# Row biases moved to quiet places of GpSimd, keys and values projected in another order over five buffers, last normalisation in four units

## The chip, the core and the metric

One NeuronCore of a Trainium2 chip runs the whole program. The metric is the device time of one execution in microseconds (us), median of three runs for the kernel before. Engines are named as the profile names them: PE is TensorE (matrix products), PEld its weight loads, DVE is VectorE, ACT is ScalarE, POOL is GpSimd, SP is the engine that only issues transfers. Each engine runs its own instructions in program order and waits on semaphores for the others.

## What is computed

Two decoder layers on x of 8 sequences, 100 tokens and 256 features, with a context of 8 times 361 rows. Each of the six blocks normalises x and adds its result to x:

```python
x = x + _L0_attn_ref(_layernorm(x), ...)     # block 0: attention ACROSS the 8 sequences, with CoPE positions
x = x + _L0_xattn_ref(_layernorm(x), ctx, ctx, ..., mask)   # block 1: single-head attention to the context
x = x + _L0_ffn_ref(_layernorm(x), ...)      # block 2: 8 experts, at most 100 tokens each, routed
x = x + _L1_attn_ref(_layernorm(x), ...)     # block 3: gated linear recurrence (a scan along the tokens)
x = x + _L1_xattn_ref(_layernorm(x), ctx, ctx, mask, ...)   # block 4: 16-head attention to the context
x = x + _L1_ffn_ref(_layernorm(x), weight)   # block 5: one product with a weight quantised to -1, 0, 1
```

The keys and values of block 4 depend on the context alone, not on x, so they can be computed at any time before block 4.

## The kernel before

Everything is written out by hand, one instruction stream per engine. `X` holds x as 100 token partitions by 8 sequences by 256; `XN` is its normalised copy, `XT` the transposed one. A normalisation is: statistics per sequence on DVE, `ve` = variance + eps on DVE, `rstd` by a power on POOL (`rsqrt`), `XN` on DVE (`norm`), transposes on PE (`transposes`), a copy to `XT` on ACT (`xt_out`). It runs in two groups of four sequences.

The row biases of blocks 0, 1, 3 and 4 are added to `X` on POOL (`bias`), and DVE adds each block's product after that (`add`).

The "side" work is the projection of block 4's keys and values: list `SIDE` gives its order, `SIDE_AT` says up to which item it has got at each named point of the program, and PE and ACT both walk the list (`side`). A key item ("k", b) is 8 matmuls of 361 columns on PE and 4 activations on ACT; then POOL splits the fp32 key into three bf16 parts (`split_key`, 3 operations), and SP stores them to `k_parts` in DRAM (`store_keys`). A value item ("v", b) is 12 matmuls and 2 activations. `k_buffer(b)` says in which SBUF buffer a key lies; a buffer is used again only when its stores have landed (`k_st`).

```python
SIDE = ([("qk", 0)] + [("k", b) for b in range(6)]
        + [("v", 0), ("k", 6), ("k", 7)] + [("v", b) for b in range(1, B)] + [("f", 0)])
SIDE_AT = {"cope": 1, "soft": 3, "ln1": 4, "b1_0": 5, "b1_2": 6, "b1_4": 7, "ln2": 8,
           "router": 9, "route": 12, "gather": 18}
```

So two keys are projected before the "spread" stage of block 0, one behind it ("ln1"), three inside the loop of block 1 ("b1_0", "b1_2", "b1_4"), and so on.

**The spread stage** (end of block 0) has 16 units u. For each, PE spreads the probabilities over the features (the product with `SELT`, 4 matmuls, line 1211), DVE multiplies by the values into `PB` (line 1660), and the sum over the 8 keys follows: on DVE for 11 units (`sum_keys`, line 484), on POOL for units 1, 4, 7, 10 and 13 (lines 706 and 707). When two units are summed, PE projects a sequence (`project0`), and DVE adds it to `X`. PE writes the spread products to `PP[u % 3]`, three pairs of PSUM banks.

**Block 1's loop** runs i from 0 to 10, a software pipeline: scores of i, transposes of i - 1, context product of i - 2, projection of i - 3, and then the side item of that i.

**Block 2** routes: POOL scatters the tokens to their experts' slots with 8 indirect transfers, SP loads the slots, PE runs the experts, SP stores `slots_out`, POOL gathers with 8 indirect transfers, DVE adds, and the normalisation for block 3 runs.

**Block 4** is driven by a table: `run_block4` walks ticks 0 to 171, and `PLAN` and `ONCE` say which piece each engine does at which tick; sequence b is 16 ticks behind sequence b - 1, and within a tick the pieces come in the sequence of `ORDER`. Block 5 follows as plain loops behind it.

## Time and profile before

| | us |
|---|---|
| median of three runs | 445.34 (443.82 to 445.56) |
| the profiled execution's own time | 443.37 |
| its span in the trace | 441.5 |
| PE busy | 407.4 (92% of the span) |
| DVE busy | 263.1 (60%) |
| ACT busy | 175.0 (40%) |
| POOL busy | 135.8 (31%) |
| mean granted TensorE clock | 0.973 of full |

The stages in the span: block 0 to its softmax until 64 us, the spread stage 64 to 113, block 1 until 164, routing until 190, the experts until 209, gather and normalisation until 228, block 3 until 322, block 4 until 428, block 5 until 441.5. A busy share is an average over all of these, so each stage has to be read by itself. A merged row of the timeline covers several like instructions: its start, its length from the first start to the last end, and in square brackets how long the engine was idle before and what released it.

### The profile page before, as it was taken

Reading aid. Unit: us, or ns where it says so; the run is one execution under the profiler, and the core shown is the slowest. Engines: PE = TensorE matmul, PEld = TensorE weight load, DVE = VectorE, ACT = ScalarE, POOL = GpSimd, SP = SyncE. Lnnn points to the kernel's source line nnn. Section 1 sums busy time; section 2 is a strip of 40 time slices with the busy share of each in tenths; the row PEclk is TensorE's granted clock in tenths of the full one; section 3 lists DMA queues with packets and bytes.
Section 4 is the critical chain, followed back from the end, with each engine's and each line's share of the span. In section 5 each row is a group of like instructions: output and inputs, shape, how many; then the busy total and the mean of one; then the engine's idle time right before and its main releaser. Section 6 shows DMA issues by size and latency. Waiting matters only on the chain.

```text
span 441.5 us, 7539 instructions
## 1 busy us (share of the span) xinstructions
PE 407.4 (92%) x2991; PEld 267.6 (61%) x2991; DVE 263.1 (60%) x473; ACT 175.0 (40%) x360; POOL 135.8 (31%) x183
## 2 busy tenths in 40 slices
PE   6999997894999999989979999999998999999976
PEld 2556754452656677658845555567765766666644
DVE  4149558499412363002379699995397677777324
ACT  0450450000443314523246585451205666666740
POOL 3830019332474300670562000000035473310100
PEclk9899999797899998999999999999999999999999
DMA  7994003000012279643210000018645446310002
GB/s 225 393 267 135 2 0 101 0 0 0 1 51 84 68 244 378 274 129 107 67 29 0 0 1 1 0 32 185 177 128 136 121 105 154 100 44 2 3 1 76
DMA packets 32850, 42.19 MB, mean 96 GB/s; under 512 B 7712, under 2 KB 29132, under 8 KB 32418
## 3 DMA queue, kind: packets, MB, share of 16 engines
q1 hardware_dynamic: 29897, 34.18, 25.5%
q0 software_dynamic: 2304, 5.76, 5.1%
q10 hardware_dynamic: 614, 1.77, 1.9%
q8 instruction: 24, 0.39, 0.4%
q14 instruction: 11, 0.09, 0.1%
HBM read 33.00 MB, written 8.98 MB: 95 GB/s over the span
## 4 chain that ended last, share of the span: by engine, by line
PE 61%; DVE 20%; issue 6%; ACT 5%; POOL 5%; DMA 3%; SPq 0%; POOLq 0%; DVEq 0%; ACTq 0%
PE banks L1073 6%; PE banks L1494 5%; PE banks L1479 4%; PE banks L1374 4%; PE banks L1448 4%; PE banks L1113 4%; PE banks L1135 4%; PE banks L1102 3%; DVE RA L484 3%; DVE NM L1848 2%; PE banks L1160 2%; PE banks L1244 2%; PE banks L1262 2%; PE banks L1342 2%; PE banks L1062 2%
## 5 line engine op out<-in xcount | busy, mean ns | idle before, releaser
L1848 DVE TENSOR_REDUCE NM<-banks 100x2 f32<-100x722 f32 x64 | 56.4, 903 | 19.4 <-PE banks L1448 19.1
L1342 PE MATMUL banks<-XT,RBG 128*128 128x400 f32 x192 | 65.0, 500 | 1.6 <-ACT XT L809 1.6
L1342 PEld LDWEIGHTS banks<-XT,RBG 128*128 128x128 f32 x192 | 36.3, 190 | 29.7 <-ACT XT L809 1.2
L1021 ACT ACTIVATE CT<-banks 128x400 f32<-128x400 f32 (+1 forms) x72 | 35.8, 504 | 23.2 <-PE banks L1479 21.7
L809 ACT ACTIVATE XT<-banks 128x800 f32<-128x800 f32 x10 | 8.3, 838 | 61.6 <-PE banks L1062 61.6
L1374 PE MATMUL banks<-W,RC 128*100 128x256 f32 x128 | 30.7, 380 | 0.6 <-DVE RC L1744 0.6
L752 POOL TENSOR_TENSOR rstd<-ve,mhalf 100x2 f32<-100x2 f32 x4 | 2.8, 702 | 88.2 <-DVE ve L1816 88.2
L1606 DVE TENSOR_TENSOR RC<-RV 128x800 f32<-128x800 f32 x16 | 15.6, 1022 | 16.1 <-ACT RV L851 14.1
L1211 PE MATMUL banks<-RC,SELT 128*128 128x400 f32 x64 | 24.3, 526 | 1.0 <-DVE RC L1646 0.7
L641 POOL TENSOR_TENSOR rstd<-ve,mhalf 100x4 f32<-100x4 f32 x10 | 10.6, 1065 | 46.3 <-DVE ve L1558 46.3
L1374 PEld LDWEIGHTS banks<-W,RC 128*100 128x100 f32 x128 | 21.0, 167 | 6.2 <-DVE RC L1744 1.0
L679 POOL TENSOR_TENSOR RA<-RA 128x722 f32<-128x722 f32 x6 | 9.1, 1510 | 49.5 <-ACT RA L831 49.5
L1102 PE MATMUL banks<-CT,W 128*128 128x361 f32 x64 | 23.2, 513 | 1.1 <-issue 1.1
L1494 PE MATMUL banks<-CT,RV 128*17 128x100 f32 (+1 forms) x576 | 24.0, 254 | 0.0
L1549 DVE BATCH_NORM_STATS2 st<-X 100x6 f32<-100x256 f32 x48 | 19.5, 423 | 7.0 <-DMA X<-in_x 5.9
L1120 PE MATMUL banks<-onesb 128*128 128x512 bf16 x81 | 21.4, 412 | 2.4 <-POOL onesf L629 2.4
L1113 PE MATMUL banks<-W,CT 128*128 128x256 f32 (+1 forms) x96 | 21.3, 380 | 0.5 <-DVE RC L1727 0.5
L1073 PE MATMUL banks<-W,RA 128*100 128x256 f32 x32 | 11.2, 485 | 10.6 <-DVE X L1588 6.1
L1727 DVE TENSOR_TENSOR RC<-banks,RC 100x256 f32<-100x256 f32 x8 | 3.4, 425 | 28.5 <-PE banks L1331 28.5
L1660 DVE TENSOR_TENSOR RC<-banks,RV 128x800 f32<-128x800 f32 x16 | 15.5, 977 | 7.6 <-PE banks L1211 7.6
L1113 PEld LDWEIGHTS banks<-W,CT 128*128 128x128 f32 (+1 forms) x96 | 17.5, 184 | 4.0 <-DVE RC L1727 0.9
L1211 PEld LDWEIGHTS banks<-RC,SELT 128*128 128x128 f32 x64 | 12.6, 201 | 11.0 <-DVE RC L1660 1.4
(244 smaller groups left out, 843.9 us busy)
## 6 DMA issues: line engine op xcount, KB each, us to landing
RA<-in_L_ffn_W SPq DMA_DIRECT2D x2, 2048.0 KB, 12.4
k_parts<-RA SPq DMA_DIRECT2D x18, 180.5 KB, 3.4
RBG<-in_L_attn_W_aiv SPq DMA_DIRECT2D x1, 3072.0 KB
CT<-in_ctx_t SPq DMA_DIRECT2D x2, 1444.0 KB, 11.4
RA<-k_parts SPq DMA_DIRECT2D x12, 180.5 KB, 3.4
RBG<-k_parts POOLq DMA_DIRECT2D x12, 180.5 KB, 4.3
RA<-k_parts POOLq DMA_DIRECT2D x12, 180.5 KB, 3.8
RBG<-in_ctx SPq DMA_DIRECT2D x2, 1024.0 KB, 17.5
```

The lines of the kernel that those rows point to most:

```text
L1021: sc.activation(P4[slot][0:n, g * HG * T:(g + 1) * HG * T], PS[4 + w % 2][0:n, 0:HG * T], ACT.Exp).then_inc(st_exp, 1)
L1073: ins = mm(bank[0:T, 0:D], lhs(k), rhs(k), start=(k == 0), stop=(k == KT - 1))
L1102: ins = mm((lo, hi)[m][:, 0:S], W4[:, 0, k, m * P:(m + 1) * P], CT[:, k, b * S:(b + 1) * S], start=(k == 0), stop=(k == KT - 1))
L1113: ins = mm(o, CT[:, k, b * S + s0:b * S + s0 + n], W4[:, 1, k, :], start=(k == 0), stop=(k == KT - 1))
L1120: mm(bank[:], onesb[:], onesb[:].unsqueeze(1).broadcast_to([P, 4, P]), start=True, stop=True)
L1135: ins = mm(PS[4 + i % 2][:, 0:GC], W0[:, w, k, m * P:(m + 1) * P], XT[:, k, GC * g:GC * g + GC], start=(k == 0), stop=(k == KT - 1))
L1211: ins = mm(PS[2 * (u % 3) + g][:, 0:GC], SELT[:, u], AL[:, GB * g:GB * g + GB].rearrange("p s t -> p (s t)"), start=True, stop=True)
L1342: ins = mm(PS[2 * aiv_pair(j, w) + g][:, 0:GC], WA[:, k, c:c + P], XT[:, k, GC * g:GC * g + GC], start=(k == 0), stop=(k == KT - 1))
L1374: ins = mm(PS[MIX_BANK[p]][0:T, b % 2 * D:b % 2 * D + D], UU[:, j, b, 1:TP], WMIX[:, j, :], start=(j == 0 and b % 2 == 0), stop=(j == RT - ...
L1494: ins = mm(PS[6][32 * c:32 * c + VW, g * T:g * T + T], V4[0:n, NJ * b + j, h, :], P4[(NJ * b + j) % PSLOTS][0:n, h * T:h * T + T], start=( ...
L1549: v.bn_stats(st6[:, b], X[:, b]).then_inc(stats_done, 1)
L1848: v.tensor_reduce(NM[:, b % 2, 2 * i:2 * i + 2], PP[w % 2][0:T, :, 0:S], AX.X, ALU.max, negate=True).then_inc(mx_out, 1)
```

## The change

- **Biases.** `bias(0)` is now issued on POOL ahead of the first `split_key`, where it was behind the second. `bias(3)`, one operation on 8 sequences, is now four on 2 sequences each, piece p behind the scan of feature group p (`state` at p + 1).
- **Side work.** All keys come first, then all values. There are five key buffers (`W0`'s space is the fifth), so four keys are ready before block 1. Keys 2 and 3 are projected in four halves inside the spread stage (`half_key`), in banks 4 and 5, which leaves the spread products two pairs of banks. Block 1's loop has no side item. The place of value 0 behind block 1 goes to key 5, the routing stage holds four values where it held two, and the gather four where it held five; 24 of 30 `keep_warm` matmuls in the routing stage go.
- **POOL's order.** In the spread stage `split_key(1)`, `(2)` and `(3)` stand between the sums. The power for the first group of block 3's normalisation stands ahead of the last gather.
- **SP's order.** The expert weights load when block 0 is done, where before six keys had to be stored; `WMIX` loads in the middle of the experts' stores.
- **Block 3's start.** PE transposes the second group after two of the three half products of the first group, not after three.
- **Last normalisation and block 5.** In four units of sequences, `LAST`, placed by tick in `ONCE`: the first six sequences' normalisation, transposes and part of the products lie inside block 4.

```diff
+LAST = [(0, 4), (4, 6), (6, 7), (7, 8)]
...
-        for r, at in ((SELT[:].rearrange("p a b -> p (a b)"), 0), (RC, 4600)):
+        for r, at in ((SELT[:].rearrange("p a b -> p (a b)"), 0), (RC, 4600),
+                      (W0[:].rearrange("p a k d -> p (a k d)"), 0)):
...
-        SIDE = ([("qk", 0)] + [("k", b) for b in range(6)]
-                + [("v", 0), ("k", 6), ("k", 7)] + [("v", b) for b in range(1, B)] + [("f", 0)])
+        SIDE = ([("qk", 0)] + [("k", b) for b in range(B)] + [("v", b) for b in range(B)] + [("f", 0)])
...
-        SIDE_AT = {"cope": 1, "soft": 3, "ln1": 4, "b1_0": 5, "b1_2": 6, "b1_4": 7, "ln2": 8,
-                   "router": 9, "route": 12, "gather": 18}
-        SIDE_LOW = [1, 9, 11, 13, 15]
+        SIDE_AT = {"cope": 1, "soft": 3, "spread": 5, "ln1": 6, "ln2": 7, "router": 8, "route": 13, "gather": 18}
+        SIDE_LOW = [1, 3, 4, 8, 10, 12, 14, 16]
+        SPREAD_AT = {4: (3, 0), 5: (3, 1), 9: (4, 0), 10: (4, 1)}
...
+                + [("last_norm", 142, 0), ("last_norm", 145, 1), ("last_tr", 146, 0), ("last_xt", 146, 0),
+                   ("last_mm", 150, 0), ("last_tr", 152, 1), ("last_xt", 152, 1), ("last_mm", 154, 1),
+                   ("last_mm", 162, 2), ("last_norm", 163, 2), ("last_tr", 169, 2), ("last_xt", 169, 2),
+                   ("last_mm", 169, 3), ("last_mm", 171, 4), ("last_norm", 171, 3), ("last_mm", 171, 5),
+                   ("last_mm", 171, 6), ("last_tr", 171, 3), ("last_xt", 171, 3), ("last_mm", 171, 7)])
...
+        K_BUFFER = (0, 1, 0, 1, 2, 3, 4, 2)
+        K_BEFORE = {2: 0, 3: 1, 7: 4}
...
-            for b in range(6):
+            for b in range(4):
                 store_keys(b)
...
-                sp.wait_ge(k_st[i], 16 * 3 * 3)
+                sp.wait_ge(k_st[i], 16 * 3 * 2)
...
-            sp.dma_start(WMIX, a["L1_attn_W_mix"].rearrange("(k p) n -> p k n", p=P)).then_inc(ld["wmix"], 16)
+            store_keys(4)
...
+            store_keys(5)
             sp.wait_ge(scat, 16 * B)
...
+                elif e == 4:
+                    sp.wait_ge(k_st[4], 16 * 3)
+                    sp.dma_start(WMIX, a["L1_attn_W_mix"].rearrange("(k p) n -> p k n", p=P)
+                                 ).then_inc(ld["wmix"], 16)
...
-            for b in range(2):
-                split_key(b)
             bias(0)
+            split_key(0)
 
             for i, u in enumerate(SUM_POOL):
...
+                if i == 0:
+                    split_key(1)
+                elif i in (1, 3):
+                    split_key(2 + i // 2)
...
-            split_key(2)
+            split_key(4)
             bias(1)
-            for b in range(3, 6):
-                split_key(b)
             rsqrt(2)
+            split_key(5)
...
-            rsqrt(3, 0)
+                if b == B - 2:
+                    rsqrt(3, 0)
...
-            bias(3)
+            for p in range(B // 2):
+                pool.wait_ge(xn_ready, 4 * B)
+                pool.wait_ge(state, p + 1)
+                gp.tensor_tensor(X[:, 2 * p:2 * p + 2], X[:, 2 * p:2 * p + 2],
+                                 RB[:, ROWBIAS[3]].unsqueeze(1).broadcast_to([T, 2, D]), ALU.add
+                                 ).then_inc(bias_added, 1)
...
+            def half_key(i, m):
+
+                b = SIDE[i][1]
+                if m == 0:
+                    pe.wait_ge(side_out, side_before(i))
+                for k in range(KT):
+                    ins = mm(PS[side_bank(i) + m][:, 0:S], W4[:, 0, k, m * P:(m + 1) * P],
+                             CT[:, k, b * S:(b + 1) * S], start=(k == 0), stop=(k == KT - 1))
+                if m == 1:
+                    ins.then_inc(side_mm, 1)
+                done[0] = SIDE_AT["spread"]
...
-                if u >= 3:
-                    pe.wait_ge(spread_used, u - 2)
+                if u >= 2:
+                    pe.wait_ge(spread_used, u - 1)
...
+                if u in SPREAD_AT:
+                    half_key(*SPREAD_AT[u])
...
-            keep_warm(PS[0], 30)
+            keep_warm(PS[0], 6)
...
-            transposes(3 * B, 1)
+                if n == 1:
+                    transposes(3 * B, 1)
```

PE's instructions in the spread stage of the kernel before; the product with SELT is line 1211, `project0` is the one with RA, and a key would be `CT,W`:

```order
L1211 MATMUL banks<-RC,SELT 128x400 x12
L1073 MATMUL banks<-W,RA 100x256 x2
L1211 MATMUL banks<-RC,SELT 128x400 x4
L1073 MATMUL banks<-W,RA 100x256 x2
L1211 MATMUL banks<-RC,SELT 128x400 x4
```

The same place in the changed kernel, where the spread product is line 1255 and a half key is line 1241:

```order
L1255 MATMUL banks<-RC,SELT 128x400 x10
L1241 MATMUL banks<-CT,W 128x361 x2
L1255 MATMUL banks<-RC,SELT 128x400 x2
L1105 MATMUL banks<-W,RA 100x256 x2
L1241 MATMUL banks<-CT,W 128x361 x2
L1255 MATMUL banks<-RC,SELT 128x400 x4
```

Keys 2 and 3 now stand between the spread products; each row counts instructions as written, of which PE runs two passes.

POOL's instructions at the same place before (line 679 to 681 is a key split, 669 the bias, 706 and 707 a sum):

```order
L696 TENSOR_SCALAR mk<-mk 8x361
L679 TENSOR_TENSOR RA<-RA 128x722
L680 CAST RA<-RA 128x722
L681 TENSOR_TENSOR RA<-RA 128x722
L679 TENSOR_TENSOR RA<-RA 128x722
L680 CAST RA<-RA 128x722
L681 TENSOR_TENSOR RA<-RA 128x722
L669 TENSOR_TENSOR X<-X,RB 100x2048
L706 TENSOR_TENSOR RC<-RC 128x400
```

And in the changed kernel (bias line 683, split 693 to 695, sum 719 and 720):

```order
L710 TENSOR_SCALAR mk<-mk 8x361
L683 TENSOR_TENSOR X<-X,RB 100x2048
L693 TENSOR_TENSOR RA<-RA 128x722
L694 CAST RA<-RA 128x722
L695 TENSOR_TENSOR RA<-RA 128x722
L719 TENSOR_TENSOR RC<-RC 128x400
L719 TENSOR_TENSOR RC<-RC 128x200
L720 TENSOR_TENSOR RA<-RC 128x100
L693 TENSOR_TENSOR RA<-RA 128x722
```

The bias now stands right behind the masks, and the first sum has one split ahead of it in place of two splits and the bias.

The end of PE's program before (1509 transposes the last attention output's sums, 1517 the output, 1073 with PEM is block 4's last projection, with WN block 5's):

```order
L1494 MATMUL banks<-SELT,RV 17x100 x16
L1509 MATMUL banks<-identf,WQK 100x113 x4
L1517 MATMUL banks<-identf,zrow 128x100 x2
L1073 MATMUL banks<-W,PEM 100x256 x2
L1062 MATMUL banks<-identf,XN 128x100 x8
L1073 MATMUL banks<-WN,XT 100x256 x8
```

And in the changed kernel (1582 is `last_tr`, 1597 `last_mm`):

```order
L1541 MATMUL banks<-SELT,RV 17x100 x12
L1556 MATMUL banks<-identf,WQK 100x113 x4
L1597 MATMUL banks<-WN,XT 100x256 x2
L1564 MATMUL banks<-identf,zrow 128x100 x2
L1582 MATMUL banks<-identf,XN 128x100 x2
L1597 MATMUL banks<-WN,XT 100x256 x2
L1105 MATMUL banks<-W,PEM 100x256 x2
L1597 MATMUL banks<-WN,XT 100x256 x6
L1582 MATMUL banks<-identf,XN 128x100 x2
L1597 MATMUL banks<-WN,XT 100x256 x2
```

Behind block 4's last projection stand four of block 5's eight products and one transposed sequence, where there were eight products and eight transposed sequences.

## Rows read from the trace of the kernel before

**Rows 1.** The page's chain that ended last, share by engine.

```profile
PE 61%; DVE 20%; issue 6%; ACT 5%; POOL 5%; DMA 3%; SPq 0%; POOLq 0%; DVEq 0%; ACTq 0%
```

**Rows 2.** Busy times by stretch: PE, PEld, DVE, ACT, POOL, then granted clock, DMA share, GB/s.

```profile
64.00:113.00 49.00, 37.41 (x114) 21.30 (x113) 41.07 (x58) 1.97 (x5) 23.87 (x23) 0.84 0.07 23
...
123.00:164.00 41.00, 40.26 (x215) 27.96 (x216) 15.65 (x48) 14.12 (x45) 16.16 (x11) 1.00 0.34 107
...
238.00:301.00 63.00, 62.60 (x197) 36.38 (x195) 58.03 (x62) 37.64 (x52) 0.00 (x0) 1.00 0.08 16
...
403.00:422.00 19.00, 18.18 (x317) 12.35 (x318) 7.10 (x18) 13.64 (x32) 1.83 (x5) 1.00 0.01 4
```

**Rows 3.** Timeline of the spread stage: start, length, engine, line, operation.

```profile
71.89 1.88 DVE L1660 TENSOR_TENSOR RC<-banks,RV 128x800 f32<-128x800 f32 x2
...
77.00 1.72 POOL L706 TENSOR_TENSOR RC<-RC 128x400 f32<-128x400 f32 x2
...
79.35 2.00 PE L1073 MATMUL banks<-W,RA 128*100 128x256 f32 x4 [4.51 <-POOL RA L707]
...
83.99 0.99 DVE L1660 TENSOR_TENSOR RC<-banks,RV 128x800 f32<-128x800 f32 x1 [5.53 <-PE banks L1211]
...
86.00 2.85 PE L1211 MATMUL banks<-RC,SELT 128*128 128x400 f32 x8
```

**Rows 4.** The chain that ended last, in block 1's loop: start, length, what.

```profile
124.91 2.62 PE banks L1102 x8
...
149.91 1.21 PE banks L1244 x4
...
154.02 1.21 PE banks L1244 x4
```

**Rows 5.** POOL beside DVE: two timeline rows, then single lines' durations (min/median/max ns).

```profile
64.05 1.56 POOL L679 TENSOR_TENSOR RA<-RA 128x722 f32<-128x722 f32 x1 [32.96 <-ACT RA L831]
...
64.62 1.84 DVE L1646 TENSOR_TENSOR RC<-RC,RA 128x800 f32<-128x800 f32 x1
...
L669 POOL TENSOR_TENSOR X<-X,RB x3: 4514/4530/4532, 72.5 to 230.0; 100x2048 f32<-100x2048 f32 x3
...
L1751 DVE TENSOR_SCALAR RA<-RA x10: 369/576/4540, 230.3 to 285.9; 128x800 f32<-128x800 f32 x6, 128x400 f32<-128x400 f32 x4
...
L1606 DVE TENSOR_TENSOR RC<-RV x16: 977/991/1271, 26.7 to 43.4; 128x800 f32<-128x800 f32 x16
...
L769 POOL TENSOR_TENSOR X<-X,RB x4: 1266/1270/1277, 336.0 to 356.4; 100x512 f32<-100x512 f32 x4
```

**Rows 6.** Timeline of one key activation on ACT, of the gather, and of block 3's start.

```profile
62.07 0.55 ACT L830 ACTIVATE RA<-banks,CB 128x361 f32<-128x361 f32 x1
...
209.53 13.22 PE L1113 MATMUL banks<-W,CT 128*128 128x256 f32 x60 [0.52 <-DVE RC L1727]
...
222.62 1.22 POOL L641 TENSOR_TENSOR rstd<-ve,mhalf 100x4 f32<-100x4 f32 x1
...
223.88 1.38 DVE L1563 TENSOR_SCALAR XN<-X,mv,rstd 100x256 f32<-100x256 f32 x4 [0.40 <-POOL rstd L641]
...
225.96 0.85 PE L1062 MATMUL banks<-identf,XN 100*128 100x100 f32 x8
...
233.84 16.39 PE L1342 MATMUL banks<-XT,RBG 128*128 128x400 f32 x48 [0.99 <-ACT XT L809]
```

**Rows 7.** Timeline of the end.

```profile
426.97 1.11 PE L1073 MATMUL banks<-W,PEM 128*100 128x256 f32 x4 [0.67 <-ACT PEM L1042]
...
428.12 0.42 DVE L1588 TENSOR_TENSOR X<-X,banks 100x256 f32<-100x256 f32 x1 [2.26 <-PE banks L1073]
...
435.13 3.70 PE L1073 MATMUL banks<-WN,XT 128*100 128x256 f32 x16 [0.99 <-ACT XT L809]
...
438.86 0.42 DVE L1588 TENSOR_TENSOR X<-X,banks 100x256 f32<-100x256 f32 x1 [0.44 <-PE banks L1073]
```

More of the change, by code:

```diff
@@ L241, in build @@
         fixed_st = sem("fixed_st")
-        k_st = [sem(f"k_st{i}") for i in range(4)]
+        k_st = [sem(f"k_st{i}") for i in range(5)]
         scat = sem("scat")
@@ L425, in run_block4 @@
                     for n, at, x in ONCE:
-                        if n == name and name in own and tick == at:
-                            own[name](x)
+                        if (n == name or n.startswith(name + "_")) and n in own and tick == at:
+                            own[n](x)
         def load_queries(queue, p, i):
@@ L586, in _ @@
             for i in (2, 3):
-                sp.wait_ge(k_st[i], 16 * 3)
+                sp.wait_ge(k_st[i], 16 * 3 * K_BUFFER.count(i))
             sp.wait_ge(fixed_st, 32)
@@ L795, in _ @@
                     bias_pair(3)
-            rsqrt(5)
+            for u, (b0, b1) in enumerate(LAST):
+                pool.wait_ge(unit_var, B // 2 + u + 1)
+                gp.tensor_tensor(rstd[:, b0:b1], ve[:, b0:b1], mhalf[:, 0:b1 - b0], ALU.pow).then_inc(unit_rstd, 1)
         @block.scalar
@@ L871, in _ @@
             side("soft")
+            side("spread")
             xt_out(xn_tr, G, xt_ready, [0])
@@ L1569, in after @@
                     return
+                if L == 4:
+                    last_stats(b)
+                    return
                 stats(L + 1, b)
@@ L1580, in after, with last_norm, last_stats @@
                     norm(L + 1, 1)
+            def last_norm(u):
+                dve.wait_ge(unit_rstd, B // 2 + u + 1)
+                for b in range(*LAST[u]):
+                    v.tensor_scalar(XN[:, b], X[:, b], mv[:, b, 0:1], rstd[:, b:b + 1], ALU.subtract, ALU.mult
+                                    ).then_inc(xn_ready, 1)
+            def last_stats(b):
+                stats(5, b)
+                if b >= 1 and b not in (b0 for b0, _ in LAST):
+                    aggregate(5, b - 1)
+                for u, (b0, b1) in enumerate(LAST):
+                    if b == b1 - 1:
+                        aggregate(5, b)
+                        dve.wait_ge(aggregated, 5 * B + b1)
+                        v.tensor_scalar(ve[:, b0:b1], mv[:, b0:b1, 1], EPS, None, ALU.add).then_inc(unit_var, 1)
             def add(L, b, bank):
@@ L1859, in normalise, with last_add @@
                                 ).then_inc(on_ready, 1)
+            def last_add(b):
+                dve.wait_ge(y5_mm, b + 1)
+                o = PS[(0, 1, 0, 1, 2, 3, 0, 1)[b]]
+                v.tensor_tensor(X[:, b], X[:, b], o[0:T, 0:D], ALU.add).then_inc(x_final, 1)
             run_block4(maxima=row_max, normalise=normalise, add=lambda b, _: add(4, b, Y4), x_add=x_add,
-                       zero_bank=zero_bank, ln_stats=ln_stats, ln_norm=ln_norm)
-            for b in range(B):
-                add(5, b, PS[4 + b % 4])
+                       zero_bank=zero_bank, ln_stats=ln_stats, ln_norm=ln_norm,
+                       last_mm=last_add, last_norm=last_norm)
 _OUT = (B, T, D)
```

106 lines of the change are left out of this document (64 added, 42 removed).

## The prediction

> **What bounds the kernel now.** I read the chain that ended last first, since a busy share of 92% for PE says nothing about one stage. It gives PE 61% and DVE 20%, with ACT and POOL at 5% each [rows 1]. The stretches [rows 2] then show four different limits. In the spread stage (64 to 113 us) DVE is busy 41.1 of 49 us, PE 37.4, at a granted clock of 0.84. In block 1's loop (123 to 164) PE is busy 40.3 of 41 and DVE 15.7: whatever leaves PE there shortens the program. In block 3 (238 to 301) DVE is busy 58.0 of 63 and is the limit that its own order sets. In block 4's tail (403 to 422) PE is busy 18.2 of 19 and ACT 13.6.
>
> The spread stage has one hole [rows 3]. POOL's first sum starts only at 77.00, behind two key splits and the bias. PE needs that sum for its first projection, so it sat idle 4.51 us until 79.35. When it came back, that projection took 2.00 us for four matmuls, against 3.70 for sixteen at the full clock [rows 7]: after the idle time the clock stood at the lower of its levels. DVE waited 5.53 us in all, until 83.99, for unit 6.
>
> **Spread stage, 3.0 us less.** The first sum now has one split ahead of it; three operations of at most 1.56 us [rows 5] are 4.7 us, and they start at the same 64.05, so POOL is free at about 68.7, and the sum of unit 1 follows its product at about 70.5. A sum takes 1.72 plus some 0.4 us [rows 3]. It is ready at about 72.6, before PE asks. What is late next is PE's queue, which now holds half keys, and with two pairs of banks it may start unit u only when unit u - 2 has been read. Unit 2 is read at 71.89 + 0.94 = 72.8 [rows 3]. Behind it on PE: unit 4 (1.4, half of 2.85 [rows 3]), half a key (1.3, half of 2.62 [rows 4]), unit 5 (1.4), the projection (0.93, a quarter of 3.70 [rows 7]), half a key (1.3), unit 6 (1.4). Together 7.7 us, so DVE gets unit 6 at about 80.7 and not at 83.99: 3.3 us earlier. In the rest of the stage DVE needs 2.4 to 3.3 us per unit, PE at most 1.4 + 1.3 + 0.93 = 3.6 with a half key and 2.4 without, so PE keeps up but for some 0.3 us at units 10 to 12. The other splits (4.7 us each) stand between sums that are 7 us apart. I take 3.0. Bounds: 5.5, the whole wait, and 0, if PE's queue or its clock eats it.
>
> **Block 1, 7.4 us less.** Three keys leave the loop; in the chain they stand as rows of line 1102, the first 2.62 us and two more of 2.45 and 2.43 [rows 4]. PE is the limit there, and a step without a key takes 154.02 - 149.91 = 4.11 us, of which the profile shows PE at work nearly throughout. Hence all three count, less 0.1. What DVE and ACT do per step is far below 4 us (15.7 and 14.1 of 41 [rows 2]). The bias of block 1 takes 4.5 us on POOL behind one split; DVE wants it at step 3, some 7 us behind step 0, and it starts before step 0: still covered. Bounds: 7.5, and 5 if the short first steps, which have little PE work, turn to waiting on ACT's exponentials.
>
> **Behind block 1, 0.4 us more.** Key 5 stands where a value stood. Its four activations take 0.55 each [rows 6], at most 2.2 us, and the copy of `XT` for the router queues behind them on ACT; a value has two. Between 0 and 1.2; I take 0.4. The two further values in the routing stage, 2.6 us each (13.22 / 5 [rows 6]), take the place of 24 warming matmuls and lie in the wait for the scattered slots: nothing.
>
> **Gather to block 3, 1.6 us less.** One value fewer frees PE 2.6 us earlier. The next limit is the normalisation: XN's first group is written from 223.88 to 225.26, PE transposed it from 225.96 [rows 6]. The power waited on POOL behind the last gather and started at 222.62; ahead of it, it may start up to 0.5 earlier. So transposes at about 224.8, 1.1 us earlier. The second group's transposes now come one half product sooner, and that half product covers ACT's copy, for which PE sat 0.99 us [rows 6]; against it the last gather starts 1 us later. I count 0.5 net. Bounds: 0 and 2.6. `WMIX` (1 MB) now goes ahead of the last expert stores in SP's queue. In block 1 the transfers made 107 GB/s at a share of 0.34, so some 315 GB/s are possible and it takes 3.3 us, with two pairs of experts still to be computed behind its issue: 0.2 us, bounds 0 and 3.3.
>
> **The biases, 1.5 us more.** POOL and DVE do disturb each other. At 64.05 POOL starts a 1.56 us subtraction, and DVE's product at 64.62 takes 1.84 us where 0.99 is usual [rows 5]: it ends 0.85 us behind POOL's end at 65.61, as if it had stood still until then. The clamp of line 1751, 369 ns at best, once took 4540 ns, when the 4.53 us bias of block 3 ran [rows 5]. That wait disappears, but ACT's table loads were the limit at that time, so it gives nothing. The four new pieces, 1.27 us each [rows 5], start when a scan ends; one product later (about 1 us, as at 83.99 [rows 3]) DVE runs an operation with both inputs in SBUF, which would stand for 0.3 to 0.4 us. Four times: 1.2 us taken, bounds 0 and 1.7. The bias of block 0 now runs beside the sixteen multiplications of line 1606, 0.99 us each, from 26.7 [rows 5]. A full stop costs DVE 4.5 us, but its five buffers put it four units (3.9 us) ahead of PE, which leaves 0.3 us taken, bounds 0 and 1.0 if the lead isn't full.
>
> The Trainium skill ("SBUF — State Buffer", section "Who interferes with whom") says of this that a VectorE instruction with two SBUF inputs contends with a GpSimd instruction that reads SBUF, and that the one that starts first holds the shared port for its whole length. By that rule, this change puts four pieces and one whole bias beside just such instructions, and the trace agrees in the row at 64.62.
>
> **The end, 2.8 us less.** Now 441.5 - 428.12 = 13.4 us pass from the last addition of block 4 to the end [rows 7], with eight products (0.93 each) and two copies in between. In the changed kernel the path is: addition 0.42, statistics to variance some 0.8, power at most 1.2, one normalised sequence 0.35 (a quarter of 1.38), transposes 0.2, copy some 0.5, product 0.93, with handovers about 4.6 us to the last addition, whose start stood 2.6 us before the end [rows 6, 7]. That is 7.2: 6.2 us less. Against this, transposes and products move ahead into a stretch where PE is busy 18.2 of 19 us: two transposes (0.85 and about 0.4) and two products (0.93 each) are 2.9 us more, and in the gaps of the last sequence (0.67 us before 426.97 [rows 7]) a third and a fourth product overrun by 0.5. Net 2.8. Bounds: 5 (ACT is the true limit in that tail and PE's additions hide) and 0.
>
> **Sum.** -3.0 - 7.4 + 0.4 - 1.6 + 0.2 + 1.5 - 2.8 = -12.7 us. The profiled execution took 443.4, so 430.7; the median of the runs shown is 2.0 above it, so about 432.5.
>
> **Rivals.** (A) The forecast, 0.63. (B) Block 1's loop doesn't get its 7.4 us back, because the shortened steps wait for ACT and DVE: 4 us are lost, 436.5. For it: step i + 1 needs step i's exponentials. Against it: PE is at work 40.3 of 41 us there [rows 2]. 0.1. (C) The port: the pieces of the biases, and the splits that now lie beside DVE's work, stop DVE at each meeting, with their bounds (1.7 + 1.0) and another 1.5 in the router: 435.5. This is the skill's rule at full price; the row at 64.62 speaks for it, the 1606 line, whose longest is 1271 ns beside two POOL operations, against it. 0.12. (D) More than forecast: the end gives 5 and the spread stage 4.5: 428.5. For it, the better clock once the idle 4.5 us is gone (0.84 now). 0.12. (E) Slower than before: the two bank pairs tie PE to DVE's reads, PE gets a pause in each unit, and its clock stays at the lower level for the stage. PE needs 35 us there at full speed (37.4 less what the low clock added, plus 5.2 for the keys); at half speed up to 70, against 49 in all. To lose the other 10 us it must run over 23 us of the stage slow. The one fall seen came behind a pause of 4.5 us, and the new queue has none over 1 us: 0.03, 447 or more.
>
> **Numbers.** 432.5 is A's. Its own range, 429.5 to 435.5; with B, C and D the range is 428 to 437. Differences under 0.5% (2.2 us) can't be told from no change: faster 0.95, same 0.02, slower 0.03.
>
> **What would show it.** Spread stage: no PE wait over 1 us before unit 6, DVE's wait there some 2.2 us, clock above 0.95. Block 1's loop: 33.6 us where it took 41. Line 1751's longest near 0.6 us, and four of DVE's line-1775 products at 1.3 us or more. From block 4's last addition to the end 7.2 us. The prediction is wrong if PE waits for ACT in block 1's first steps, if the experts' last store lands late behind `WMIX`, or if block 4's tail grows by more than 3.4 us.

## The result, and the profile after

The changed kernel took 439.2 us (median of 4 runs, 437.58 to 443.51); the kernel before, beside it, 445.45 us. The ratio is 0.9866, with a 95% interval of 0.9831 to 0.9901. The forecast was faster, which holds (by 1.3%), by 12.7 us, which doesn't: some 6 us came. The profiled execution took 437.58 us with a span of 435.8, against 443.4 and 441.5 before, so the two traces differ by 5.7 us, and that is what has to be divided up. Executions of one kernel fall into a fast and a slow state: ratios use the fast ones alone and medians all of them, and the traces of experiments 2 and 3, which are of slow ones, are read for single stretches only.

The windows of the changed kernel, over the stretches that answer to those of [rows 2] (mean granted clock, then DMA share and GB/s, stand last):

```profile
62.00:111.00 49.00, 42.32 (x139) 24.30 (x138) 43.43 (x61) 8.98 (x18) 26.97 (x28) 0.97 0.15 46
120.00:154.00 34.00, 32.83 (x191) 23.29 (x192) 15.53 (x48) 8.80 (x33) 4.86 (x2) 1.00 0.20 59
232.00:294.00 62.00, 60.83 (x192) 35.34 (x190) 56.04 (x56) 36.09 (x50) 5.09 (x4) 1.00 0.09 18
398.00:422.00 24.00, 22.10 (x360) 15.33 (x361) 8.67 (x22) 15.72 (x36) 2.74 (x6) 1.00 0.03 7
```

The spread stage has its clock back (0.97 for 0.84), and block 1's loop takes 34 us for 41 with PE nearly as full as it was (32.8 of 34 us, 40.3 of 41). To see where the rest went, I took one event at each border in both traces and subtracted:

| stretch, up to | before, us | after, us | change | forecast |
|---|---|---|---|---|
| DVE's reduction of block 0's logits | 59.24 | 60.15 | +0.9 | +0.3 |
| last spread product | 105.25 | 103.09 | -3.1 | -3.0 |
| first scores of block 1 | 123.19 | 120.64 | -0.4 | 0 |
| last projection of block 1 | 163.33 | 153.44 | -7.3 | -7.4 |
| first gather | 212.32 | 202.87 | +0.4 | +0.6 |
| first full product over the scans (line 1775, now 1862) | 242.03 | 234.21 | +1.6 | -1.6 |
| last scan | 299.32 | 292.94 | +1.4 | +1.2 |
| last addition of block 3 | 337.0 | 332.2 | +1.6 | 0 |
| end | 441.5 | 435.8 | -0.9 | -2.8 |

The two large terms are right to 0.1 us. Of the 7.0 us that are missing, 3.2 went between the gather and block 3, 1.6 at block 3's end, 1.9 in the tail, 0.6 in block 0; the other rows give 0.3 back.

**The hole in the spread stage**, in the changed kernel's timeline (answers to [rows 3]):

```profile
71.48 1.72 POOL L719 TENSOR_TENSOR RC<-RC 128x400 f32<-128x400 f32 x2 [1.92 <-DVE RC L1747]
77.84 1.03 PE L1105 MATMUL banks<-W,RA 128*100 128x256 f32 x4
81.46 0.99 DVE L1747 TENSOR_TENSOR RC<-banks,RV 128x800 f32<-128x800 f32 x1 [2.02 <-PE banks L1255]
```

POOL's first sum starts at 71.48 and no longer at 77.00, PE's projection waits for nothing and takes 1.03 us for four matmuls instead of 2.00, and DVE waits 2.02 us for unit 6, where it waited 5.53.

**Between gather and block 3** (answers to [rows 6]):

```profile
212.81 1.04 POOL L655 TENSOR_TENSOR rstd<-ve,mhalf 100x4 f32<-100x4 f32 x1 [0.98 <-DVE ve L1625]
213.89 3.38 DVE L1630 TENSOR_SCALAR XN<-X,mv,rstd 100x256 f32<-100x256 f32 x4
214.08 1.18 POOL L748 DMA_INDIRECT XN<-slots_out,small  x1 [0.23 <-issue]
214.36 0.72 PE L1094 MATMUL banks<-identf,XN 100*128 100x100 f32 x4 [2.44 <-DVE XN L1630]
215.44 1.69 POOL L761 MEMSET CT<- 128x808 f32 x2
216.47 0.39 PE L1094 MATMUL banks<-identf,XN 100*128 100x100 f32 x2 [1.40 <-DVE XN L1630]
219.00 5.28 PE L1388 MATMUL banks<-XT,RBG 128*128 128x400 f32 x8 [0.22 <-ACT XT L833]
```

Four normalisations that took 1.38 us took 3.38; PE waited 2.44 and 1.40 us in its transposes, and its next 8 multiplications took 0.66 us each, where those of before took 0.36 (4.27 us for 12).

**Block 3 and its end.** Source line 1862, one of POOL's pieces, and PE where the last scan releases it:

```profile
L1862 DVE SCALAR_TENSOR_TENSOR RC<-RA,RC x4: 999/1178/1361, 244.9 to 290.9; 128x808 f32<-128x808 f32 x4
269.89 1.27 POOL L768 TENSOR_TENSOR X<-X,RB 100x512 f32<-100x512 f32 x1 [6.60 <-DVE RC L1831]
270.65 1.36 DVE L1862 SCALAR_TENSOR_TENSOR RC<-CT,RC 128x808 f32<-128x808 f32 x1
294.83 6.25 PE L1421 MATMUL banks<-W,RC 128*100 128x256 f32 x20 [2.00 <-DVE RC L1831]
```

Half of the eight products took 1.36 us, as forecast. New is the last row: PE sat idle for 2.00 us and then took 6.25 us for 20 matmuls that had taken 4.56. The same row before, line 1374 there, has a pause of 0.62 us:

```profile
301.21 4.56 PE L1374 MATMUL banks<-W,RC 128*100 128x256 f32 x20 [0.62 <-DVE RC L1744]
```

**The tail** (answers to [rows 7]; rows of PE):

```profile
417.63 1.11 PE L1597 MATMUL banks<-WN,XT 128*100 128x256 f32 x4
421.84 1.11 PE L1597 MATMUL banks<-WN,XT 128*100 128x256 f32 x4
426.80 1.03 PE L1597 MATMUL banks<-WN,XT 128*100 128x256 f32 x4
427.67 1.03 PE L1105 MATMUL banks<-W,PEM 128*100 128x256 f32 x4
432.04 1.11 PE L1597 MATMUL banks<-WN,XT 128*100 128x256 f32 x4 [0.43 <-ACT XT L1075]
```

Block 4's last product (line 1105) now comes at 427.67, behind a product of block 5 at 426.80. From it to the end 8.2 us pass, where it was 14.6; but from block 3's last addition to it 95.5 us pass, where it was 90.0.

### The profile page after: what moved, and what is told of

Read it like the earlier page. It is cut to its first block, busy times and chain, and to the rows that moved or that the text cites. A ratio compares the mean times of both kernels' runs of the same rounds, so it can differ in the third digit from the quotient of the medians.

```text
span 435.8 us, 7507 instructions
## 1 busy us (share of the span) xinstructions
PE 405.3 (93%) x2967; PEld 265.5 (61%) x2967; DVE 267.7 (61%) x475; ACT 174.9 (40%) x362; POOL 137.1 (31%) x188
## 4 chain that ended last, share of the span: by engine, by line
PE 56%; DVE 22%; issue 7%; DMA 5%; ACT 5%; POOL 3%; SPq 1%; POOLq 0%; DVEq 0%; ACTq 0%
PE banks L1421 5%; PE banks L1541 4%; PE banks L1105 4%; PE banks L1167 4%; PE banks L1526 4%; PE banks L1495 3%; PE banks L1255 3%; DVE NM L1934 3%; PE banks L1192 3%; PE banks L1388 2%; PE banks L1290 2%; PE banks L1308 2%; DVE RA L493 2%; DVE RC L1862 2%; DVE RC L1828 2%
## 5 line engine op out<-in xcount | busy, mean ns | idle before, releaser
L1388 PE MATMUL banks<-XT,RBG 128*128 128x400 f32 x192 | 67.3, 513 | 0.2 <-ACT XT L833 0.2
L1388 PEld LDWEIGHTS banks<-XT,RBG 128*128 128x128 f32 x192 | 37.4, 196 | 29.6 <-issue 3.1
L1421 PE MATMUL banks<-W,RC 128*100 128x256 f32 x128 | 32.3, 395 | 2.0 <-DVE RC L1831 2.0
L1693 DVE TENSOR_TENSOR RC<-RV 128x800 f32<-128x800 f32 x16 | 19.3, 1278 | 14.2 <-ACT RV L875 14.2
L655 POOL TENSOR_TENSOR rstd<-ve,mhalf 100x4 f32<-100x4 f32 x8 | 8.5, 1057 | 47.8 <-DVE ve L1625 47.8
L768 POOL TENSOR_TENSOR X<-X,RB 100x512 f32<-100x512 f32 x4 | 5.1, 1272 | 45.5 <-DVE RC L1831 45.5
L1152 PE MATMUL banks<-onesb 128*128 128x512 bf16 x57 | 16.7, 435 | 2.4 <-POOL onesf L643 2.4
L1134 PE MATMUL banks<-CT,W 128*128 128x361 f32 x48 | 17.7, 521 | 1.1 <-issue 1.1
L1526 PE MATMUL banks<-RC,RA 100*128 100x100 bf16 (+1 forms) x192 | 16.6, 210 | 1.3 <-DMA RC<-NT 1.3
L833 ACT ACTIVATE XT<-banks 128x800 f32<-128x800 f32 x8 | 6.6, 841 | 27.9 <-PE banks L1094 27.9
```

Source lines behind the costliest of these rows:

```text
L1134: ins = mm((lo, hi)[m][:, 0:S], W4[:, 0, k, m * P:(m + 1) * P], CT[:, k, b * S:(b + 1) * S], start=(k == 0), stop=(k == KT - 1))
L1388: ins = mm(PS[2 * aiv_pair(j, w) + g][:, 0:GC], WA[:, k, c:c + P], XT[:, k, GC * g:GC * g + GC], start=(k == 0), stop=(k == KT - 1))
L1421: ins = mm(PS[MIX_BANK[p]][0:T, b % 2 * D:b % 2 * D + D], UU[:, j, b, 1:TP], WMIX[:, j, :], start=(j == 0 and b % 2 == 0), stop=(j == RT - ...
L1526: ins = mm(PS[4 + w % 2][0:n, c * T:c * T + T], KS[b % KSLOTS][0:KROWS, h, s0:s0 + n], queries(KROWS, h, b), start=True, stop=True)
L1693: v.tensor_tensor(PB[u % 5], k0[:, k].rearrange("p (s t) -> p s t", s=B), q0[:, k, s * T:s * T + T].unsqueeze(1).broadcast_to([P, B, T]), ...
```

## The experiments

Each kernel is the changed one with the edit shown. I read the local stretch from its trace first, since single edits are worth 1 to 3 us and the executions of one kernel lie up to 15 us apart. Each experiment has one trace.

**1. PE kept busy ahead of the transposes** (439.2 became 438.3; ratio to before 0.9885, 0.9809 to 0.9960)

```diff
-            keep_warm(PS[2], 5)
+            keep_warm(PS[2], 17)
```

> The changed kernel with 17 warming matmuls, where it has 5, ahead of the transposes of XN's first group between the gather and block 3; nothing else. In the changed kernel PE stopped at 211.9, waited 2.44, 1.40 and 0.46 us in and before those transposes, and then took 5.28 us for the first 8 multiplications of W_aiv (0.66 each, where 0.356 is the pace of the kernel before: 4.27 us for 12). Theory 'the clock': what lowered it is the idle 2.4 us, so with it filled the first 8 take 2.9 to 3.3 us and the whole comes 2 us earlier (437.2 where the changed kernel took 439.2). Theory 'the normalisation': the 1.40 and 0.46 us inside the transposes are enough to keep the clock low, or the first half of W_aiv isn't on the path: the 8 still take over 4.5 us or the median stays within 0.5 us of 439.2.

```profile
214.25 3.38 DVE L1630 TENSOR_SCALAR XN<-X,mv,rstd 100x256 f32<-100x256 f32 x4
219.36 3.65 PE L1388 MATMUL banks<-XT,RBG 128*128 128x400 f32 x8 [0.22 <-ACT XT L833]
293.57 4.56 PE L1421 MATMUL banks<-W,RC 128*100 128x256 f32 x20 [2.01 <-DVE RC L1831]
```

The 8 multiplications take 3.65 us, the normalisation 3.38 as without the edit, and from the first gather to the first full product 29.8 us pass, not 31.3: this much of the clock's share is worth 1.6 us. It is not all of it: the granted clock was still 0.50 from 217.4 to 220.8, and the 8 took more than the 2.9 to 3.3 us that were expected. The median says nothing at this size. The third row is a warning: the pause at block 3's end is there as in the changed kernel, and this time the clock held.

**2. The power behind the last gather** (436.7 us; 0.9761, 0.9692 to 0.9831)

```diff
-                if b == B - 2:
-                    rsqrt(3, 0)
+            rsqrt(3, 0)
```

> The changed kernel with the power of block 3's first group back behind POOL's last gather, as it stood in the kernel before. In the changed kernel the four normalisations of that group took 3.38 us from 213.89, where 1.38 is usual, with the last gather's issue (1.18 us) and two memsets (1.69 us) on POOL at the same time. Theory 'POOL stops DVE, gather first': without the gather beside it the group takes 1.4 to 1.8 us and is ready at 216.2 or earlier, in place of 217.27; the transposes end 1 us earlier, and the median falls by 0.5 to 1 us. Rival 'the memsets do it': they now begin right behind the power and lie beside the whole group; it takes 2.5 us or more and nothing is won, or 0.3 us lost.

```profile
217.54 2.56 DVE L1629 TENSOR_SCALAR XN<-X,mv,rstd 100x256 f32<-100x256 f32 x4 [0.40 <-POOL rstd L655]
217.65 1.67 POOL L760 MEMSET CT<- 128x808 f32 x2
```

Without the gather beside it the group still takes 2.56 us, with the memsets at the same time: that is what the rival expected of the group. Its price was wrong, though: the stretch is 30.1 us and not 31.3 or more.

**3. The memsets behind the normalisation** (432.7 us; 0.9748, 0.9699 to 0.9798)

```diff
+            pool.wait_ge(xn_ready, 3 * B + GB)
             gp.memset(DEC[:, :, :, 0:1], 0.0)
```

> The changed kernel with POOL's memsets ahead of block 3 behind the normalisation of XN's first group, and nothing else. Of the stretch from the first gather to DVE's first full-width scan product (31.3 us; 29.7 before) the warming alone took 1.6 us away, the power alone 1.2, all three edits 4.0. If the three add up, this one takes 1.2 us away: 30.1 us, the four normalisations 2.4 us or less where they took 3.4. Rival 'the gather's issue is what stops DVE, the memsets only follow it': they still take over 3 us, and the three edits gave more together than apart because only together do they leave the clock up.

```profile
213.78 1.42 DVE L1631 TENSOR_SCALAR XN<-X,mv,rstd 100x256 f32<-100x256 f32 x4
213.89 1.22 POOL L748 DMA_INDIRECT XN<-slots_out,small  x1 [0.23 <-issue]
215.12 0.47 DVE L1819 SCALAR_TENSOR_TENSOR X<-XN,small,X 100x256 f32<-100x256 f32 x1
215.52 1.65 POOL L762 MEMSET CT<- 128x808 f32 x2
216.72 4.62 PE L1389 MATMUL banks<-XT,RBG 128*128 128x400 f32 x8 [0.64 <-ACT XT L834]
```

No expectation had this: the group takes 1.42 us beside the gather's issue, so without the memsets nothing holds it, and one wait is worth 3.0 us (28.3 for 31.3) even with the clock still low in the last row. The three edits overlap, they don't add up. One detail stays open: in the changed kernel the third of the four normalisations is recorded from 214.54 to 216.42, and the first memset only from 215.27. That taking the memsets away frees it is shown; why it stood 0.7 us ahead of them is not.

**4. All three, with 20 warming matmuls** (431.4 us; 0.9710, 0.9665 to 0.9755)

> The changed kernel with three edits between the gather and block 3: the power of XN's first group behind the last gather, POOL's five memsets behind that group's normalisation, and 20 warming matmuls instead of 5. Nothing is then beside the normalisation, and PE has no pause. With the power alone moved, the normalisation took 2.56 us; with the warming alone, 1.6 us of this stretch came back. Theory 'two causes, POOL beside the normalisation and PE's clock': the four normalisations take 1.4 us and the 8 multiplications behind them 2.9 us; from the first gather to DVE's first full-width scan product (line 1862) 28.0 to 28.8 us pass, where the changed kernel took 31.3 and the one before 29.7. Rival 'one cause is all': 29.5 to 29.9, as with the warming alone.

```profile
214.56 1.38 DVE L1630 TENSOR_SCALAR XN<-X,mv,rstd 100x256 f32<-100x256 f32 x4 [0.40 <-POOL rstd L655]
217.47 2.92 PE L1388 MATMUL banks<-XT,RBG 128*128 128x400 f32 x8 [0.64 <-ACT XT L833]
```

Both at full speed, and 27.3 us for the stretch: 4.1 less than in the changed kernel, 2.4 less than before, where the forecast said 1.6. Each edit alone leaves 1.0 to 2.8 us of that.

**5. Block 3's bias whole again** (433.8 us; 0.9777, 0.9722 to 0.9832). One operation over all sequences at its old place instead of the four pieces.

> The changed kernel with block 3's bias as one operation of 4.5 us at its old place, and not as four pieces behind the scans. In the changed kernel four of DVE's products of line 1862 took 1.37 us where 1.00 is usual (1.44 us in all), DVE's last scan ended 6.38 us earlier than before and PE's multiplications 7.77 us earlier, PE then sat idle for 2.00 us at 292.83 and took 6.25 us for 20 matmuls of W_mix (4.56 before). Theory 'the pieces cost twice': they delay DVE by 1.4 us, which opens PE's pause, which lowers its clock: without them the products take 1.00 us, the pause is 0.6 us, the clock in that stretch 1.0, and the median falls by 2.5 to 3 us. Rival 'the clock falls for itself': 1.4 us are won and the 20 matmuls still take over 5.5 us. Rival 'the whole bias costs as much': the clamp waits up to 4.5 us for it and ACT's table loads no longer hide it: less than 1 us is won.

```profile
L1859 DVE SCALAR_TENSOR_TENSOR RC<-RA,RC x4: 999/999/999, 243.3 to 287.8; 128x808 f32<-128x808 f32 x4
291.73 4.56 PE L1418 MATMUL banks<-W,RC 128*100 128x256 f32 x20 [0.60 <-DVE RC L1828]
```

All products take 1.00 us, the pause is 0.60 and the 20 matmuls 4.56. From the first full product to block 3's last addition 94.9 us pass (232.6 to 327.5), where it was 98.0: 3.1 us, twice what the pieces cost DVE. The clamp took 4.09 us once and cost nothing, hidden under ACT's table loads as forecast.

**6. The bias of block 0 earlier** (441.6 us; 0.9906, 0.9866 to 0.9946). `bias(0)` ahead of the wait for the masks.

> The changed kernel with the bias of block 0 ahead of POOL's wait for the masks, where POOL sat idle for 5.47 us (20.99 to 26.46), and not beside the sixteen multiplications of line 1693. Theory 'the bias stops DVE': the multiplications' mean falls from 1278 ns to 1000 to 1080, the chain up to the spread stage ends 0.5 to 0.9 us earlier, and the median falls by as much. Rival 'the second mask operation and the earlier start of the key splits do it': the mean stays above 1200 ns with the bias away. A third outcome: the row biases' transfer lands later than 21, and the bias still meets the multiplications.

```profile
27.36 5.09 POOL L683 TENSOR_TENSOR X<-X,RB 100x2048 f32<-100x2048 f32 x1 [5.55 <-DMA BR<-in_L_ffn_br]
L1693 DVE TENSOR_TENSOR RC<-RV x16: 975/978/5315, 26.2 to 44.6; 128x800 f32<-128x800 f32 x16
```

The third outcome: the row biases' transfer held POOL until 27.36, and the bias met the multiplications all the same. But the second row shows what a meeting is: one multiplication of sixteen took 5.3 us, and the median 978 ns. It is recorded from 27.98 to 33.30, and the bias ends at 32.45: DVE isn't slowed, it stands until POOL has finished and ends 0.85 us later.

**7. Block 5 back behind block 4** (440.2 us; 0.9910, 0.9871 to 0.9949). The last units undone, the rest as changed.

> The changed kernel with one part undone: block 5's normalisation, transposes and products stand behind block 4 in two groups of four, as in the kernel before; the rest is as changed. The last units put five PE steps ahead of block 4's last product (420.31, 427.67) and shortened what follows its addition from 13.4 to 7.0 us. Theory 'the tail is PE's': those steps each cost their full time (0.87, 0.93, 0.56, 0.93, 1.0 us; by the two traces 5.1 us lost against 6.4 won), so with the part undone the tail from block 4's last product to the end is 14.5 us again, block 4 ends 4 to 5 us earlier, and the whole ends 1.3 us later than the changed kernel, as it did in the profile. Rival 'the forecast': the part is worth 2.8 us, and the 1.08 us that PE waited for a transfer of the maxima has nothing to do with it: 2.5 to 3 us later.

```profile
422.14 1.11 PE L1091 MATMUL banks<-W,PEM 128*100 128x256 f32 x4 [0.67 <-ACT PEM L1060]
430.29 3.70 PE L1091 MATMUL banks<-WN,XT 128*100 128x256 f32 x16 [0.99 <-ACT XT L826]
```

From block 3's last addition (331.4) to block 4's last product 90.7 us pass, 95.5 in the changed kernel; from there to the end (436.7) 14.6 for 8.2. So the units lose 4.8 and win 6.4: 1.6 us net in these two traces, between the two expectations. PE's waits for the maxima's transfers are in it, 0.4 us here and 1.3 in the changed kernel; without them the net is 2.5.

**8. Eight pieces, and the end reordered** (436.7 us; 0.9831, 0.9772 to 0.9890)

```diff
-            for p in range(B // 2):
...
+            for b in range(B):
+                pool.wait_ge(state, b + 1)
+                ins = gp.tensor_tensor(X[:, b], X[:, b], RB[:, ROWBIAS[3]], ALU.add)
...
-                   ("last_mm", 162, 2), ("last_norm", 163, 2), ("last_tr", 169, 2), ("last_xt", 169, 2),
-                   ("last_mm", 169, 3), ("last_mm", 171, 4), ("last_norm", 171, 3), ("last_mm", 171, 5),
-                   ("last_mm", 171, 6), ("last_tr", 171, 3), ("last_xt", 171, 3), ("last_mm", 171, 7)])
+                   ("last_norm", 162, 2), ("last_mm", 162, 2), ("last_tr", 169, 2), ("last_xt", 169, 2),
+                   ("last_mm", 171, 3), ("last_mm", 171, 4), ("last_norm", 171, 3), ("last_mm", 171, 5),
+                   ("last_tr", 171, 3), ("last_xt", 171, 3), ("last_mm", 171, 6), ("last_mm", 171, 7)])
```

> The changed kernel with two edits far apart. (1) Block 3's bias in eight pieces of one sequence each (0.64 us), one behind each scan, and not four of 1.27 us. DVE's operation right behind a scan reads a PSUM bank and took 0.96 us beside a piece as without one; the product of line 1862 comes 0.91 us behind the scan and was held until the piece's end. Theory 'DVE stands until POOL's operation ends, and only where both its inputs are in SBUF': a piece of 0.64 us ends before it, all eight products take 1.00 us, PE's pause is 0.6 us and the 20 matmuls behind it 4.56. Rival 'any meeting costs': the products or the scans take 0.2 us or more longer. (2) At the end, block 5's fourth product behind block 4's last and not ahead of it, and the normalisation of the third unit ahead of the third addition. Expected: block 4's last product (427.67 there) 0.8 us earlier against block 4's eighth reciprocal, and the end 0.8 us nearer; the rival says the products behind it then hold the last unit's transposes and nothing is won.

```profile
268.29 0.96 DVE L1860 TENSOR_TENSOR RC<-RC,banks 128x800 f32<-128x800 f32 x1
268.46 0.73 POOL L768 TENSOR_TENSOR X<-X,RB 100x256 f32<-100x256 f32 x1 [6.79 <-DVE RC L1831]
269.29 1.00 DVE L1862 SCALAR_TENSOR_TENSOR RC<-CT,RC 128x808 f32<-128x808 f32 x1
293.12 4.56 PE L1421 MATMUL banks<-W,RC 128*100 128x256 f32 x20 [0.59 <-DVE RC L1831]
```

A piece of 0.73 us ends at 269.19 under DVE's operation on a PSUM bank, and the product behind it takes 1.00 us: the same bias, in smaller pieces, is free. At the end 7.7 us pass from the last reciprocal (421.25) to the last addition (428.97), where it was 8.3: 0.6 us won of 0.8.

**9. All edits** (428.1 us; 0.9631, 0.9582 to 0.9680). Experiments 4 and 8, and `bias(0)` behind `pool.wait_ge(pos_ready, 1)`.

> Everything that the runs so far point to: the gather edits (power, memsets, warming), block 3's bias in eight pieces, the end's two edits, and the bias of block 0 behind DVE's sum over the gates (about 52 us), where DVE's operations read PSUM banks, and not at 30 us, where it stopped one multiplication of line 1693 for 5.3 us. Against the changed kernel I expect 0.9 us from the bias of block 0 (0 if DVE's operations at 52 to 57 stop too), 2.5 to 3 from the gather stretch, 1.4 and the 1.6 of the low clock from block 3's bias, 0.8 from the end: 6 to 7.5 us, so 432 to 433.5 us. If the theory of two causes is wrong at any of these places, the trace shows it there.

```profile
L1694 DVE TENSOR_TENSOR RC<-RV x16: 978/988/1266, 26.7 to 43.4; 128x800 f32<-128x800 f32 x16
51.24 0.99 DVE L1716 TENSOR_TENSOR RC<-RC,banks 128x800 f32<-128x800 f32 x1
51.29 4.57 POOL L683 TENSOR_TENSOR X<-X,RB 100x2048 f32<-100x2048 f32 x1 [21.14 <-DVE RC L1703]
52.21 3.46 DVE L1722 TENSOR_TENSOR RA<-RA,banks 128x700 f32<-128x700 f32 x7
```

The multiplications are what they were before [rows 5], block 0's reduction is at 59.2 again (0.9 us won), and the 4.57 us bias lies beside eight operations with a PSUM input, none of which is longer than without it. The sum was 6 to 7.5 us; 11 came against the changed kernel's median. The span of the profiled execution fell by 9.6, which the stretches account for: 0.9, 4.1 (27.2 for 31.3), 3.0 in block 3 (95.0 for 98.0) and 1.6 in the tail, of which 1.1 is less waiting for the maxima.

**10. And one product moved into a pause** (426.6 us; 0.9657, 0.9579 to 0.9734). `("last_mm", 154, 1)` became `("last_mm", 160, 1)`.

> The kernel with all edits, and block 5's second product moved from between block 4's last products (tick 154) to the pause behind its last weighted sums (tick 160), where PE waits some 0.7 us for ACT's copy. Theory 'the tail is PE's, and only its pauses are free': from block 4's seventh product to its eighth 0.7 us less (6.4 us in the kernel with all edits), and the end comes as much earlier against the last reciprocal's stage. Rival: DVE's addition then stands ahead of the last reciprocal and delays it: nothing is won or up to 0.4 us lost.

From block 4's seventh product to its eighth 5.56 us pass (409.63 to 415.19), and 6.36 in experiment 9 (411.29 to 417.65): 0.8 us. The ratios of 9 and 10 can't be told apart.

**11. One key back in block 1's loop** (447.1 us; 1.0054, 1.0014 to 1.0093)

```diff
-        SIDE_AT = {"cope": 1, "soft": 3, "spread": 5, "ln1": 6, "ln2": 7, "router": 8, "route": 13, "gather": 18}
+        SIDE_AT = {"cope": 1, "soft": 3, "spread": 5, "ln1": 6, "b1_2": 7, "ln2": 7, "router": 8, "route": 13, "gather": 18}
```

> The changed kernel with one key projection (key 5) back in block 1's loop, behind its third step, and none behind block 1. The forecast's largest term was that PE is the limit in the loop and each of three keys there counts in full (2.45 us), and that behind block 1 a key is nearly free (0.4 us dearer than the value it replaced). By that, the stretch from the first projection of the loop to the last grows by 2.4 to 2.5 us, what is behind it shrinks by 0.4, or by up to 2.5 if the key that stands there now costs its full length too, and the first gather comes 2.0 us later than in the changed kernel (0 if it costs its full length in either place). Rival 'the loop waits for ACT and DVE': the stretch grows by less than 1.5 us.

```profile
127.40 2.62 PE L1134 MATMUL banks<-CT,W 128*128 128x361 f32 x8
159.36 1.56 POOL L693 TENSOR_TENSOR RC<-RC 128x722 f32<-128x722 f32 x1
159.43 4.34 DVE L1630 TENSOR_SCALAR XN<-X,mv,rstd 100x256 f32<-100x256 f32 x4 [1.13 <-POOL rstd L655]
161.12 0.39 PE L1094 MATMUL banks<-identf,XN 100*128 100x100 f32 x2 [3.53 <-DVE XN L1630]
164.23 5.39 PE L1325 MATMUL banks<-WR,XT 128*100 128x8 f32 x32
```

From the loop's first scores to its last projection 35.26 us pass (120.53 to 155.79), and 32.80 in the changed kernel: 2.46, as forecast. But the first gather comes 8.9 us later, not 2.0. With key 5 done early, POOL splits it at 159.36, just when DVE normalises, and the group takes 4.34 us for 1.38. PE, without the key, waits 3.53 us, and the router's 32 matmuls take 5.39 us where they took 3.08 (1.50 and 1.58). These two steps make 5.3 of the 8.9 us, the loop 2.3; the other 1.3 come later. The key that stood there was more than free: it kept POOL away from DVE. Whether it also kept the clock up isn't shown: the granted clock fell at 162.2 or 162.3 in both traces, until 165.7 in the changed kernel, whose router was through by 162.0, and until 172.4 here. That is one trace; the median, 7.9 us above the changed kernel's, agrees with it.

## Why the prediction was right and where it failed

**Right.** The spread stage (-3.1 for -3.0) by the very steps forecast: first sum at 71.5, unit 6 at 81.5 (80.7 forecast, and block 0 came 0.9 later), no wait of PE's over 1 us before it, clock 0.97. One reading was short: the forecast knew one fall of the clock in this stage, behind the pause of 4.51 us, but the kernel before had two (granted clock 0.52 from 77.0 to 84.0 and 0.51 from 104.0 to 114.5), so the 0.84 was not that pause's alone. Also right: block 1 (-7.3 for -7.4): PE is the limit, and experiment 11 prices a key there at 2.46. `WMIX` and key 5 (+0.4 for +0.6). Block 3's pieces as far as DVE goes (+1.4 for +1.2). The tail behind block 4's last addition (428.73 to 435.8: 7.1 for 7.2).

**Gather to block 3: +1.6 where it said -1.6.** The failed step is "transposes at about 224.8, 1.1 us earlier". It let the normalisation take its 1.38 us whenever it came. Counted from the first gather, ACT's copy behind the transposes came 0.6 us later and not 1.1 earlier (15.15 for 14.59). In the kernel before, POOL's memsets started at 225.09, when PE had finished its side projections, and the normalisation ended at 225.26:

```profile
225.09 0.33 POOL L741 MEMSET RA<- 128x64 f32 x1 [1.24 <-PE banks L1106]
```

With one value fewer PE is ready long before, the memsets follow the gather at once and fall on the normalisation. Experiment 3 shows that: one wait, 1.42 us for 3.38, 3.0 us. The second part is the clock: PE, freed earlier, got a pause of 2.44 us, and the next multiplications ran at half speed (experiments 1 and 4; with the pause filled and the memsets away, 2.92 us for 5.28). I had counted PE's freedom as gain alone; it started POOL's work and stopped PE's clock.

The forecast named the Trainium skill's rule ("SBUF — State Buffer", section "Who interferes with whom") for the pieces, and not here. The same section of the Trainium skill says that a VectorE instruction in a two-port mode, which `tensor_scalar` can enter, contends with GpSimd, and that one with two SBUF inputs contends only with a GpSimd instruction that reads. The traces agree on both: the normalisation (`tensor_scalar`) stood where memsets followed and not where they were held back (experiment 3), while an addition with two SBUF inputs that began inside the same memsets took 0.45 us in experiment 9:

```profile
215.15 1.65 POOL L762 MEMSET CT<- 128x808 f32 x2
215.69 0.45 DVE L1819 SCALAR_TENSOR_TENSOR X<-XN,small,X 100x256 f32<-100x256 f32 x1
```

The addition at 215.12 in experiment 3 began ahead of the memsets and says nothing on this.

**Block 3's end: +1.6 where it said nothing.** The pieces held DVE for 1.4 us and PE not at all, so PE's pause before the last scan grew from 0.62 to 2.00 us. In eight profiles with that pause five had the 20 matmuls at 6.25 us and three at full speed; in five without it none was slow. The whole price of the pieces was thus 1.4 us and, in five of eight traces, 1.6 more. The term "the biases, 1.5 us more" had the right stop and no eye for who waits behind DVE.

**The tail: -0.9 where it said -2.8.** The step "two transposes and two products are 2.9 us more, a third and a fourth product overrun by 0.5" was too low: 5.5 us were lost up to block 4's last product (95.5 for 90.0) where it said 3.4, the very sign that the forecast had given for being wrong, and 6.4 won behind it where it said 6.2. Two things are in the 5.5. First, the product at 426.80 stood ahead of block 4's last one, which came 2.83 us behind its reciprocal and not 1.83, a whole product later (experiments 8 and 10 win 0.6 and 0.8 by placing single products elsewhere). The forecast's own parts, 0.85, 0.4 and twice 0.93, also make 3.1 and not 2.9. Second, PE waited 1.3 us in all for transfers of the maxima, 1.1 of it at 411.12, and not at all in the profile before. That wait varies (0.2 to 1.7 us in the eleven other profiles), and it stands with the old tail of experiment 7 too (0.4), so the units alone don't make it; what sets it was not tried. With the wait taken off, 102.0 to 102.3 us pass from block 3's last addition to the end in the five traces that have the new tail unedited and no low clock in it, and 104.6 before: 2.2 to 2.6 us less. So of the 1.9 us that are missing here 1.3 are the wait, and 0.6 the step.

**Block 0: +0.9 where it said +0.3.** One multiplication stood for the bias's whole 5.1 us, so it took 4.3 us more than the usual 0.98. The lead of five buffers covered 3.4 of these; the forecast let it cover all but 0.3. From the first multiplication to the reduction 33.5 us pass, and 32.5 both before and in experiment 9, where the bias is elsewhere.

**Rivals.** B is dead (experiment 11). C gave a price of 435.5 and was nearest in kind: stops of DVE, but by a memset and in places it did not name. D wanted 5 at the end and 4.5 in the spread stage, where 0.9 and 3.1 came, and E's slow clock through the spread stage never came (0.97). With the memsets alone kept apart (experiment 3) the median was 432.7, next to the forecast of 432.5, but that is luck: the wait is worth 3.0 us in the trace, the two medians differ by 6.5, and block 3's end and block 0 were as far off as ever.

**Open.** In three of the thirteen profiles the clock stood at half speed for some 13 us at the start of block 4, as here in experiment 3:

```profile
331.00:345.00 14.00, 13.40 (x130) 9.06 (x131) 7.80 (x15) 5.06 (x11) 3.21 (x9) 0.57 0.21 55
```

It costs 5.3 to 5.6 us (21.0 to 21.2 us from block 3's last addition to the first reciprocal, 15.7 in the ten others) and would explain why executions of one kernel lie 5 us and more apart: the profiled one of experiment 3 took 439.56 us, its four others 431.48 to 433.54. A pause of PE's of 0.94 us stood right ahead of it, but it stands in profiles without a fall too. What tips it was not tried.

## What to carry to other kernels

An engine that comes free earlier sets loose everything gated on it: look up what POOL does next, and on which DVE operation it will fall, before counting the gain. Where POOL and a DVE operation that it can hold meet, DVE stops in full, so what matters is whether POOL's piece ends under a DVE operation that it can't hold, one with a PSUM input here: pieces of 1.27 us cost 0.36 each, pieces of 0.73 us nothing. Where PE is made to wait some 2 us, fill the pause; matmuls that do nothing were worth 1.6 us here.
